# Moving a weight split to GpSimd, one weight fill ahead of two exponentials, and a new order of the first attention bodies

## The reference, cut to what matters

```
x = x + 0.5 * ffn(layernorm(x))          # 8 experts of rank 16, the best two of each token
x = x + attn(layernorm(x))               # 32 heads
x = x + 0.5 * ffn(layernorm(x))

q      = rms_norm(x @ wq_a.T) @ wq_b.T                   # rank 384; per head 128 plain + 64 rotated
kv     = x @ wkv_a.T                                     # 128 compressed + 64 rotated, shared by all heads
k, v   = rms_norm(kv[:128]) @ wkv_b.T
scores = (q_plain @ k_plain + rope(q_rot) @ rope(k_rot)) * scale, causal
out    = softmax(scores) @ v @ wo.T
```

## Time and profile before

| | us |
|---|---|
| median of three runs | 2319.09 |
| the profiled execution | 2315.2 |
| its span, first to last instruction | 2313.4 |
| PE busy in it | 2266.9 |
| DVE busy | 1556.3 |
| ACT busy | 931.3 |
| POOL busy | 523.5 |

### The profile page before, as it was taken

The page is one execution under the profiler, slowest core; times in us unless marked ns, Lnnn a source line. Parts: engine busy times, 40 slices in busy tenths (PEclk is TensorE's granted clock), DMA queues, the critical chain, the costliest instruction groups (busy, mean ns, idle before and its releaser), DMA issues.

```text
span 2313.4 us, 40096 instructions
## 1 busy us (share of the span) xinstructions
PE 2266.9 (98%) x12444; PEld 1929.2 (83%) x12444; DVE 1556.3 (67%) x3587; ACT 931.3 (40%) x2313; POOL 523.5 (23%) x578
## 2 busy tenths in 40 slices
PE   8989999999999999999999999999999999999999
PEld 8968888888888888888888978888888888888888
DVE  7656666666666666667777566666666666666677
ACT  5543333443333333344454533333333333333333
POOL 4212222122221222211133222222222222222211
PEclk9999999999999999999999999999999999999999
DMA  4023333323233333333322133333333323333221
GB/s 167 6 67 114 110 110 101 108 83 88 74 101 110 105 110 110 102 109 93 102 90 78 28 85 81 80 80 80 80 80 80 80 80 80 80 80 80 77 70 74
DMA packets 216428, 203.47 MB, mean 88 GB/s; under 512 B 144176, under 2 KB 172720, under 8 KB 214320
## 3 DMA queue, kind: packets, MB, share of 16 engines
q1 hardware_dynamic: 195920, 158.65, 24.4%
q10 hardware_dynamic: 20448, 44.04, 5.7%
HBM read 97.78 MB, written 54.53 MB: 66 GB/s over the span
## 4 chain that ended last, share of the span: by engine, by line
PE 88%; DVE 5%; ACT 3%; issue 2%; DMA 1%; POOL 0%; SPq 0%; ACTq 0%; DVEq 0%; POOLq 0%
PE ps L713 74%; PE ps L1064 5%; PE ps L781 5%; PE ps L727 2%; PE ps L1020 1%; DVE arena L1596 1%; ACT arena L1226 1%; PE ps L1027 1%; DVE stage L1941 1%; DVE xacc L1953 1%; DVE negmax L1931 1%; ACT stage L1489 1%; DVE ps L1929 0%; ACT stage L1226 0%; DVE stats L1605 0%
## 5 line engine op out<-in xcount | busy, mean ns | idle before, releaser
L713 PE MATMUL ps<-arena 128*128 128x512 f32 (+1 forms) x4032 | 967.3, 380 | 5.1 <-DVE xacc L1697 2.6
L1596 DVE TENSOR_TENSOR arena<-ps,arena 128x512 fp32r<-128x512 f32 (+2 forms) x920 | 535.1, 599 | 491.6 <-ACT arena L1226 491.3
L1226 ACT ACTIVATE arena<-ps 128x512 fp32r<-128x512 f32 (+2 forms) x920 | 466.8, 526 | 763.8 <-PE ps L713 437.6
L713 PEld LDWEIGHTS ps<-arena 128*128 128x128 f32 x4032 | 670.3, 190 | 117.8 <-issue 11.1
L713 PE MATMUL ps<-zT,arena 128*128 128x512 f32 (+1 forms) x1746 | 440.8, 396 | 4.8 <-ACT ropeT L1226 4.4
L1489 ACT ACTIVATE stage<-ps,negmax 128x128 f32<-128x128 f32 (+6 forms) x512 | 259.9, 508 | 394.1 <-DVE negmax L1931 390.5
L1953 DVE TENSOR_TENSOR xacc<-ps,xacc 128x512 f32<-128x512 f32 x512 | 351.3, 686 | 79.0 <-PE ps L713 71.0
L713 PEld LDWEIGHTS ps<-zT,arena 128*128 128x128 f32 x1746 | 323.1, 189 | 77.9 <-ACT ropeT L1226 4.9
L2158 POOL TENSOR_TENSOR stage<-stage,pos_tab 128x512 f32<-128x512 f32 (+1 forms) x66 | 83.0, 1258 | 1253.7 <-ACT stage L1226 1240.7
L713 PE MATMUL ps<-keyT,arena 128*128 128x128 f32 (+6 forms) x1536 | 326.5, 321 | 3.2 <-ACT stage L1489 2.6
L713 PEld LDWEIGHTS ps<-keyT,arena 128*128 128x128 f32 x1536 | 256.1, 189 | 53.1 <-issue 19.3
(11 more groups left out here) (87 smaller groups left out, 1351.8 us busy)
## 6 DMA issues: line engine op xcount, KB each, us to landing
kept_out<-arena SPq DMA_DIRECT2D x16, 2048.0 KB, 6.3
arena<-arena SPq DMA_DIRECT2D x248, 128.0 KB, 3.0
arena<-kept_out ACTq DMA_DIRECT2D x30, 1024.0 KB, 5.8
stage<-in_wo SPq DMA_DIRECT2D x16, 1024.0 KB, 5.8
stage<-stage SPq DMA_DIRECT2D x248, 64.0 KB, 2.0
kept_q<-arena SPq DMA_DIRECT2D x16, 768.0 KB, 7.6
arena<-kept_q ACTq DMA_DIRECT2D x32, 384.0 KB, 3.5
out<-xacc SPq DMA_DIRECT2D x15, 512.0 KB, 2.6
```

What stands on the lines that cost most here:

```text
L713: last = nc.tensor.matmul(dst, w, m, start=start and n == 0, stop=stop and n == len(passes) - 1, skip_group_check=skip)
L1226: return nc.scalar.activation(dst, src, ACT.Copy)
L1596: return nc.vector.tensor_tensor(dst, src, part.bitcast(F32), ALU.subtract)
```

## The change

Four things are changed. First, the low part of `w_pe` is made by GpSimd and no longer by DVE: in the loop between GpSimd's two rotations, in the first body inside the rotation of `pf1` after its first multiplication, and before the attention behind the third root mean square. Second, in all loop bodies ACT reads a fill of place `front` ahead of the slot's first two exponentials; only `m2` in slot 2 of pair 0 has that place. Third, the first bodies are in a new order on PE, ACT and DVE: `pe1` goes ahead of slot 1's scores, the transposes of slot 0 are drawn together ahead of `q2`, `q3` comes before slot 1's transposes and `m1` between them, pair 1's `pf1` moves from before `q2` to behind slot 1's transposes, and pair 0's output (2, 2) moves ahead of two transposes. Fourth, in pair 0's first body SP issues the load of the output weights ahead of the stacking of the first half of `pe1`.

The table `FIRST`, pair 1:

```diff
-            + [["pf1", "q2", "q3", "pe0", "q0", "q1"]] * (NPAIR - 1)
+            + [["q2", "q3", "pf1", "pe0", "q0", "q1"]] * (NPAIR - 1)
```

SP, `first_body`:

```diff
-                stack_halves(turns(p, 0, 1), 1, None, 0, PART)
                 if p == 0:
                     sp.wait_ge(zckt_done, NT)
                     sp.wait_ge(lat_hi, 4 * NT)
                     sp.wait_ge(lat_lo, 4 * NT)
                     load_wo(0)
+                stack_halves(turns(p, 0, 1), 1, None, 0, PART)
```

PE, `first_body`:

```diff
                 score(0, 3)
+                fill(p, 0, "pe1", PRO[p])
                 score(1, 0)
                 score(1, 1)
-                fill(p, 0, "pe1", PRO[p])
                 score(1, 2)
                 turn_latents(n)
-                score(1, 3)
                 turn(0, 0)
                 pe.wait_ge(z_read, 2 * (n + 1))
                 turn(0, 1)
+                score(1, 3)
+                turn(0, 2)
+                turn(0, 3)
                 pe.wait_ge(lat_hi, 4 * (n + 1))
                 pe.wait_ge(lat_lo, 4 * (n + 1))
-                if p > 0:
-                    fills("pf1")
-                    turn(0, 2)
-                    turn(0, 3)
-                    fills("q2")
-                else:
-                    fills("q2")
-                    turn(0, 2)
-                    turn(0, 3)
+                fills("q2")
                 values(slot_n(p, 0, 0), 0, True)
+                fills("q3")
                 turn(1, 0)
                 turn(1, 1)
-                fills("q3")
+                fills("m1")
                 turn(1, 2)
                 turn(1, 3)
-                fills("m1")
-                fills("m3")
+                fills("m3" if p == 0 else "pf1")
                 values(slot_n(p, 0, 1), 1, False)
...
-                    outputs(2, 0, 1)
+                    outputs(2, 0, 1, 2)
                     turn(2, 0)
                     turn(2, 1)
-                    outputs(2, 2)
                     fills("pe0")
```

ACT, `body` (its `first_body` follows PE's new order):

```diff
+                    fills(k, "front")
                     exps(p, g, k, 0)
                     exps(p, g, k, 1)
-                    fills(k, "front")
```

DVE, `first_body` (which else follows PE's new order) and `slot`:

```diff
                 if p == 0:
                     maxi(2, 2)
+                    maxi(2, 3)
                     fills("m2")
-                    maxi(2, 3)
+                    adds(2, 0)
                     norms(p, 0, 2)
-                    adds(2, 0, 1)
+                    adds(2, 1)
...
-                if k == 1 and not last:
-                    split_wpe(p, g + 1)
                 norms(p, g, k)
```

POOL:

```diff
+            def split_wpe(p, g):
+                pool.wait_ge(wpe_hi, p * NG + g + 1)
+                settle(pool)
+                G.tensor_tensor(w_pe[:, 1, :], s_wpe.rearrange("p k n -> p (k n)"), w_pe[:, 0, :].bitcast(F32),
+                                ALU.subtract).then_inc(wpe_lo, 1)
...
-                    rotate(turns(p, 0, 1) + 1, qbase(p, 0) + ev["pf1"][0] + 1, c0=PART)
+                    rotate(turns(p, 0, 1) + 1, qbase(p, 0) + ev["pf1"][0] + 1, c0=PART,
+                           between=lambda: split_wpe(p, 1))
                 else:
                     rotate(turns(p, g, 1), qbase(p, g) + ev["pe1"][0] + 1)
+                if not last and not first:
+                    split_wpe(p, g + 1)
                 if not last:
                     rotate(turns(p, g, 1) + 1 + first, qbase(p, g) + ev["pe0"][0] + 1)
```

More of the change, by code:

```diff
@@ L1390, in first_body @@
                 exps(p, 0, 0, 3)
+                read_fill(p, 0, "pe1", PRO[p])
                 exps(p, 0, 1, 0)
-                read_fill(p, 0, "pe1", PRO[p])
                 exps(p, 0, 1, 1)
-                exps(p, 0, 1, 2)
-                latents(n)
                 turn(0, 0)
                 turn(0, 1)
-                if p > 0:
-                    fills("pf1")
+                latents(n)
+                turn(0, 2)
+                turn(0, 3)
+                exps(p, 0, 1, 2)
                 exps(p, 0, 1, 3)
-                if p > 0:
-                    turn(0, 2)
-                    turn(0, 3)
-                    fills("q2")
-                else:
-                    fills("q2")
-                    turn(0, 2)
-                    turn(0, 3)
+                fills("q2")
                 valued(slot_n(p, 0, 0), 0)
-                turn(1, 0)
-                turn(1, 1)
                 fills("q3")
@@ L1415, in first_body @@
                     q_weights_back(1, 1)
+                turn(1, 0)
+                turn(1, 1)
+                fills("m1")
                 turn(1, 2)
                 turn(1, 3)
-                fills("m1")
-                fills("m3")
+                fills("m3" if p == 0 else "pf1")
                 valued(slot_n(p, 0, 1), 1)
@@ L1782, in lat_step @@
                     tokens(n - 1)
-                if j == 2:
-                    split_wpe(p, 0)
                 if j + 1 < NT:
@@ L1837, in first_body @@
                 norms(p, 0, 0)
-                maxi(1, 2)
-                latents(n)
                 turn(0, 0)
                 turn(0, 1)
+                latents(n)
+                turn(0, 2)
+                turn(0, 3)
+                maxi(1, 2)
                 maxi(1, 3)
-                if p > 0:
-                    turn(0, 2)
-                    turn(0, 3)
-                    fills("q2")
-                else:
-                    fills("q2")
-                    turn(0, 2)
-                    turn(0, 3)
+                fills("q2")
                 norms(p, 0, 1)
                 o_split(slot_n(p, 0, 0), 0)
+                fills("q3")
                 turn(1, 0)
                 turn(1, 1)
-                fills("q3")
+                fills("m1")
                 turn(1, 2)
                 turn(1, 3)
-                fills("m1")
                 fills("m3")
@@ L1863, in first_body @@
                 maxi(2, 1)
-                split_wpe(p, 1)
                 if p == 0:
                     maxi(2, 2)
+                    maxi(2, 3)
                     fills("m2")
-                    maxi(2, 3)
+                    adds(2, 0)
                     norms(p, 0, 2)
-                    adds(2, 0, 1)
+                    adds(2, 1)
                     turn(2, 0)
@@ L1958, in o_split @@
                 lo(low, by_head(bank_pv), high).then_inc(o_lo, 1)
-            def split_wpe(p, g):
-                dve.wait_ge(wpe_hi, p * NG + g + 1)
-                lo(w_pe[:, 1, :], s_wpe.rearrange("p k n -> p (k n)"), w_pe[:, 0, :]).then_inc(wpe_lo, 1)
             def slot(p, g, k, last=False):
@@ L2136, in lat_step @@
                     rms_norm(n - 1)
+                if j == 2:
+                    split_wpe(p, 0)
                 if j < 5:
                     ln_lat(s, j + 3)
+            def split_wpe(p, g):
[3 more added lines that the diff above has]
+                                ALU.subtract).then_inc(wpe_lo, 1)
             def rotate(r, a_wait, first=False, between=None, c0=0, c1=SEQ):
```

## The result

The changed kernel takes 2302.10 us (median of four, 2298.64 to 2303.82), the kernel before beside it 2318.48: ratio 0.993, 95% interval [0.9915, 0.9946]. That is 16.4 us less, where 12.8 were forecast, and inside the range of 2299 to 2315. A second measurement, five runs in another group, gave 2302.52 against 2316.26, ratio 0.994 [0.9926, 0.9953], 13.7 us less. The two profiled executions stand at 2315.2 and 2298.64, their spans at 2313.4 and 2296.8.

A forecast was written before the change was run, and what follows sets the result against it. PE was taken as full in pair 1's loops, losing time in both first bodies and in pair 0's waits for DVE. Gains 5.7 + 4.0 + 2.7 + 0.4 = 12.8 us took 2319.1 to 2306.3, range 2299 to 2315 (forecast's own 2303 to 2310).

The forecast's parts named there:

- Loops of pair 0: Pair 0's 14 loop bodies: moving the split off DVE gains 0.41 us each, 5.7 us; 11.8 at best.
- the hold: Pair 0's loops: GpSimd's split keeps a DVE norm of slot 1 waiting, taken as 0.85 us.
- The forecast's own formula: Pair 0's loops: if one split holds DVE for h us, a body gains 0.84 - (h - 0.42).
- The rival of no hold: Pair 0's loops: GpSimd's split doesn't hold DVE, loops give 11.8 us, kernel at 2300.2; chance 0.15.
- that of the whole instruction: Pair 0's loops: GpSimd's split holds DVE for its whole length, loops give 3.5 us, 2308.5; chance 0.15.
- First body of pair 0 up to `pf1`: The new order and earlier load of `wo` cut PE's waits and low clock there: 4.0 us (2 to 6).
- From `pf1` on: Pair 0, `pf1` to next body: norm and addition waits go, the stack's landing then limits: 2.7 us (1.5 to 3).
- The step that named the order of the outputs as the cause: Behind pair 0's `pf1`: outputs (2, 0) to (2, 2) in a row remove both waits and slow part, about 4.3 us.
- First body of pair 1: PE gains early, but `pf1`'s later rotation and stacking give most back: 0.4 us (-1 to 2).
- The chain: Pair 1's first body: GpSimd waits for ACT's split in `pf1`'s rotation; next body starts 0.8 us earlier at best.
- the bound of -1: Pair 1's first body: lower end of the range -1 to 2 us around its forecast gain of 0.4 us.
- The sum: Whole kernel: 5.7 + 4.0 + 2.7 + 0.4 = 12.8 us less, so 2306.3 us.

The follow-up runs named there:

- c1: The changed kernel measured once more without any edit, in another group of runs: 2302.52 us, 0.994 of the kernel before.
- e3: Changed kernel, but in the loop bodies GpSimd begins its split of `w_pe` only after DVE's four norms of slot 1: 2299.49 us.
- e9: Changed kernel, but in the loops DVE makes the low part of `w_pe` again, ahead of slot 1's norms: 2301.95 us.
- e8: Changed kernel, but in pair 0's first body output (2, 2) is behind the two transposes again and DVE's additions behind its norms: 2299.73 us.
- e7: Changed kernel, but in pair 0's first body SP issues the load of `wo` behind the stack of `pe1` again: 2305.43 us.
- e4: Changed kernel, but in pair 1's first body ACT makes the high part of `w_pe` right behind its read of `pf1`: 2295.80 us.
- e5: Changed kernel with the edits of both e3 and e4: 2294.49 us, 0.991 of the kernel before.
- e6: Changed kernel, but in the 14 loop bodies of each pair GpSimd makes the same split of `w_pe` twice: 2302.46 us.

## Why the prediction was right

**Loops of pair 0: 5.7 forecast, 6.6 measured** (6.85 with c1). The mechanism is shown by e3 and the size of the hold by its norms: 0.75, the measured share of the earlier trace rows scaled by columns. I had taken 0.85. With the hold out of the way (e3) the loops are 11.3 us shorter than before, of the 11.8 that the forecast gave as the most. The forecast's own formula gives with 0.75 a gain of 0.51 a body, and the stretch gained 0.53; over the whole body 0.47 are left, since 0.06 are lost again outside the stretch; the cause is open.

What the forecast did not separate: three quarters of the gain (5.0) are ACT's new order, which cost nothing elsewhere, as forecast. The split's move gives 1.5 to 1.8; without the hold it would have been 6.2 (e9 against e3). The rival of no hold and that of the whole instruction are both out. The Trainium skill, page "SBUF — State Buffer", section "SBUF: two separate sides", has the pair held for the whole instruction. Of 1.02 us free time the norms lost 0.75, so the measurement decides. What the other 0.25 are stays open.

**First body of pair 0 up to `pf1`: 4.0 forecast**, 3.7 in the first pair of profiles. The forecast wanted 2.8 less idle time and 1.2 from the clock; idle time went from 7.17 (taken for some 6.6) to 4.18 us, 3.0 less, and busy time from 25.50 at 0.95 to 24.83 at 1.00, 0.7 less. The waits for `q2` (0.53) and `q3` (1.00) are those forecast; the load still costs 0.53, and the transposes behind `m1`, given 1 us, wait for nothing. **From `pf1` on: 2.7 forecast**, 2.6 measured, and slot 3's scores wait for the stack's landing (1.75), as forecast. But here the number was right for the wrong reason. The step that named the order of the outputs as the cause failed (e8): 1.9 of the 2.7 are PE's busy time, 14.28 at a clock of 0.90 and 12.40 at 1.00, and the rest is probably the split's move.

As a whole this body took 65.20, 67.53 and 68.49 us in the three executions with the old order, and 58.76 to 61.20 in the ten with the new one, e7 left out. The means are 67.1 and 59.7, so 7.3 in place of 6.7: the profile that the sum was made against had the shortest of the old ones. The early load is the largest known part (e7: some 5 us with the clock). Without it the body takes 64.29, which is 0.9 less than in the first profile of before and 2.8 less than the mean of the old order, and up to `pf1` PE then idles as long as before, 7.09 and 7.17 us. There the tighter order only turns other waits into a longer one for the load (3.74 in e7, 1.90 before). What the order and the split's move add to the load is 1 to 3 us. One by one these two were not tried.

**First body of pair 1: 0.4 forecast, nothing or a small loss measured.** The chain was as forecast: GpSimd idle until ACT's split, PE idle before slot 3's scores, which come 39.99 us behind the body's start where they came 41.65 behind it. What the forecast put at nothing was the clock behind that idle time. The three matmuls of 320 columns take 1.08 us behind the wait of 2.52 (0.69 before), the clock in the ten us from there is 0.83, and from slot 3's scores to the next body it is 16.62 us in place of 15.06. In all three executions with the old order that is 15.06. With the new one it is 16.55 to 16.66 in seven of nine (e4 and e5 apart); c1 and e6 kept the full clock, with 15.24 and 15.20, and only there PE waits for the last stack (0.43 and 0.35), as the forecast had it for the end of the body. The means of the body are 55.8 (three) and 56.5 (nine). The term was mis-sized by about 1 us, inside the bound of -1, and that the first two profiles differ by no more than 0.1 is luck: before's 56.71 was the longest of the old ones.

**The sum.** 7.34 - 0.67 + 6.72 = 13.4 us, against 13.7 in the second comparison of medians and 16.4 in the first. The first profile's 16.6 hold 3.0 that belong to no part of the change (c1). The forecast of 2306.3 was 4.2 too high: 0.6 of it are the terms, 0.6 the median of before (2319.1 then, 2318.5 beside the changed kernel), and 3.0 the scatter between sets of runs, which c1's group doesn't show again. What makes that scatter as a whole stays open; the clock between the pairs is one source of its size. The sum of 12.8 is right by its largest term, the loops, whose mechanism held. Its other terms came out near their numbers in part through the clock, which the forecast had counted for 1.2 us and in the slow outputs.

## What to carry to other kernels

Before moving an operation to an idle engine, look what that engine's instruction stands beside: here it stood beside four short instructions of the other engine and held them for 0.75 us, and one wait that put it behind them was worth three times the move itself. When a chain of dependent steps bounds a stretch, put no operation into its middle whose own input comes late: with that input 5 us earlier the body was 3.3 to 4.3 shorter, the more where the clock had fallen behind the wait. And compare an untouched stretch in both traces first; what it differs by is the error of all the others.

## What the runs showed of the hardware

A GpSimd instruction of 384 columns takes 1.02 us alone and 1.24 behind a norm in progress, and holds the next norm of DVE for 0.75; DVE's additions and low parts, which read PSUM, take 0.68 and 1.27 us for two beside it, as without it. The low clock is not a matter of the kernel alone: in the stretch between the pairs the same kernel showed 1.00 once and 0.87 once in the same 20 us. In pair 1's first body it fell behind PE's wait of 2.4 to 3.0 us in seven of nine executions, and not at all in e4 and e5, which have no such wait. The load of `wo` issued 6.2 us earlier took 7.5 us and not 5.1 until PE had it, so only part of the head start arrived. It had more transfers beside it (0.87 of the DMA engines' time in those ten us); whether that is the cause was not tried.
